# A DMA that adds, seven state buffers and a moved softplus in a one-core Mamba layer with experts

## The chip, the cores and the metric

The kernel runs on one core of a Trainium2 chip, as one launch. The metric is the device time in microseconds (us) from its start to its end. The engines of a core work side by side and meet only at semaphores: TensorE (PE in the profile, PEld for its weight loads), VectorE (DVE), ScalarE (ACT), GpSimd (POOL) and SyncE (SP), which here only issues loads. Sixteen DMA engines move the data.

## What is computed

A layer on x of 8 x 256 tokens with 1024 features. First an adapted projection (`cond`), then a selective state-space block with its scan over the tokens, then a second adapted projection folded into a layer of 8 low-rank experts of which each token uses 2. The scan is the part that matters here:

```
u, gate = split(cond(x) @ W_in.T)                    # 2048 channels each
u = silu(conv4(u) + conv_b)
dt, Bm, Cm = rmsnorm of the parts of u @ Wx.T        # 64, 16, 16
delta = softplus(dt @ Wdt.T + dt_bias)
state = exp(delta * A) * state + (delta * u) * Bm    # per token; 16 states per channel
y = sum over the 16 states of (state * Cm) + u * D
x = x + (y * silu(gate)) @ W_out.T
x = x + ffn(cond2(x))                                # top 2 of 8 experts of rank 64
```

All of it is float32. A matmul of 128 x 128 weights by 256 tokens stands in the trace as two rows.

## The kernel before

**Chunks.** Channels are taken 128 at a time and batch rows one at a time: 8 rows x 16 channel groups = 128 chunks, numbered `i`, with batch row `b = i // 16` and group `c = i % 16`. The 16 states of a chunk are taken in four quarters `q` of 4 states, each a tile of 128 partitions x 1024 (4 states x 256 tokens). A quarter has the number `n = 4 i + q`.

**One quarter.** GpSimd multiplies `delta * u` (`w_sb`, made once a chunk by `weight`) by the broadcast rows of B into a plane of the ring `st` (`dbu`, L1544). ScalarE writes `exp(delta * A)` into one of two PSUM tiles `scan0`, `scan1` (`decay`, L1146 and L1149). VectorE scans along the tokens in place (`scan`, L1317) and multiplies the result by the rows of C (`mul`).

**Adding the four products.** The product of q = 0 goes to its plane in `st`. That of q = 1 stays in PSUM (L1327), and `add_first` on VectorE adds the plane of q = 0 to it and writes the plane of q = 1 (L1334). The products of q = 2 and 3 go to their planes (L1329); GpSimd adds plane 1 into 2 and 2 into 3 (`add`, L1552), folds four states to two (`fold`, L1558), and TensorE sums the last two through the identity into PSUM (`sum_states`, L666). VectorE then makes `y` (`y_sum`, `y_gate`).

**The ring.** `st` has `ST_RING = 6` planes, taken round. A `dbu` may start when the plane it overwrites is free: for q = 2 that is `mul_done` of the chunk before, for q = 1 `id_mm`, TensorE's sum of two chunks earlier.

**Softplus.** `dt_proj` on TensorE leaves two channel groups (128 x 512) in a PSUM bank. ScalarE writes relu of it to `delta` and abs to `tmp` (`dt_evac`, L1032, L1033), which frees the bank, then exp and ln on `tmp` (`softplus`, L1039, L1041). GpSimd adds `tmp` to `delta` (`delta_add`, L1562). There are 64 of these, eight to a batch row.

**The other work of a chunk's turn (slot).** TensorE has in each slot a `late` job (mostly a 1024 x 256 piece of the output projection, 32 rows of the trace), a `small` and a `half` job, the sum of the chunk before, the `u` projection 20 chunks ahead and the gate projection of the next chunk (16 rows each). Each job uses one PSUM bank and waits until the job before in that bank is emptied. VectorE also does the three taps of the convolution (`conv_tap`, L1298) and adds results of the late and half jobs. Weight tiles of 512 KB go by SP into the ring `wt` of 6.

**What sets the order.** Each engine runs its own list, written out by hand in the loop over `i`; nothing is reordered. The order on VectorE in chunk `i` is: scan 0, late result, scan 1, the other results, product 0, product 1, `add_first`, scan 2, taps, scan 3, product 2, product 3, y of chunk `i - 1`. On GpSimd: `delta_add` if there is one, `weight(i + 1)`, `dbu` 0 to 2 of `i + 1`, add 2, add 3, fold of `i`, `dbu` 3 of `i + 1`.

## Time and profile before

| | us |
|---|---|
| median of 3 runs | 2437.41 (2436.84 to 2438.94) |
| time of the profiled execution | 2438.53 |
| span of its trace | 2436.6 |
| busy: PE, DVE, POOL, ACT | 2248.4, 2228.7, 2117.4, 1614.4 |
| prologue, up to the first scan | 119.7 |
| the 128 chunks | 2255.6 |
| tail, from the end of the last scan on | 61.3 |

Shares of the whole span mix a prologue with stages whose limits differ, so the table says only which engines come into question. What bounds a stretch is read from the stretch: the busy time of each engine in it, and whether an engine starts each instruction as the one before ends. Times of instructions are "start, duration"; two neighbours overlap by some 0.08 us, so the cost of one is taken from start to start.

### The profile page before, as it was taken

What the parts mean: (1) busy time and instruction counts of PE and PEld (TensorE: products, weight loads), DVE (VectorE), ACT (ScalarE), POOL (GpSimd) and SP (SyncE); (2) the same over time, 40 slices, a digit from 0 to 9 for tenths busy, and PEclk for the clock granted to TensorE, in tenths of its full rate; (3) what the DMA queues carried; (4) which work ended last, traced back from release to release, by engine and by line L of the source; (5) the groups of instructions that cost most, each with busy time, mean ns of one, the idle gap of its engine ahead of it and who ended that gap; (6) DMA issues with size and microseconds to landing.
All of it is one profiled execution on the core that took longest, in us unless ns stands there. A gap on an engine that the chain in (4) does not pass through costs nothing.

```text
span 2436.6 us, 30543 instructions
## 1 busy us (share of the span) xinstructions
PE 2248.4 (92%) x10140; PEld 1898.7 (78%) x10140; DVE 2228.7 (91%) x2104; ACT 1614.4 (66%) x3763; POOL 2117.4 (87%) x1090
## 2 busy tenths in 40 slices
PE   8999999999999999999999999999989887788879
PEld 7777878888788877888778877888768765666767
DVE  1389999999999999999999999999999999998892
ACT  1367667866677667776677667776677666765550
POOL 0189889999899999999899999999899989999870
PEclk9999999999999999999999999999989987998989
DMA  7454444433455344534454334644345332532342
GB/s 228 143 200 111 136 138 171 154 131 130 140 190 159 122 156 164 168 126 152 140 182 163 117 127 150 207 136 149 116 161 162 133 98 72 185 125 88 113 140 96
DMA packets 133178, 352.15 MB, mean 145 GB/s; under 512 B 38733, under 2 KB 43341, under 8 KB 131549
## 3 DMA queue, kind: packets, MB, share of 16 engines
q1 hardware_dynamic: 110254, 298.28, 37.1%
q10 hardware_dynamic: 22768, 51.93, 6.4%
q8 instruction: 81, 1.33, 0.2%
q14 instruction: 75, 0.61, 0.1%
HBM read 339.14 MB, written 11.02 MB: 144 GB/s over the span
## 4 chain that ended last, share of the span: by engine, by line
PE 32%; DVE 27%; POOL 19%; issue 12%; ACT 10%; ACTq 0%; DMA 0%; DVEq 0%; SPq 0%; POOLq 0%
DVE scan L1317 14%; POOL st L1544 10%; PE ubank L649 5%; POOL st L1552 5%; PE ubank L622 5%; PE late L703 5%; DVE st L1329 4%; DVE ubank L1298 3%; ACT scan L1149 3%; DVE scan L1327 3%; ACT L1238 3%; PE scan L622 2%; PE gbank L601 2%; ACT L1153 2%; POOL st L1558 1%
## 5 line engine op out<-in xcount | busy, mean ns | idle before, releaser
L1544 POOL TENSOR_TENSOR st<-w_sb,bc 128x1024 f32<-128x1024 f32 x512 | 1199.0, 2357 | 113.7 <-PE gbank L666 100.8
L1317 DVE TENSOR_TENSOR_SCAN scan<-scan,st 128x1024 f32<-128x1024 f32 x512 | 1167.5, 2288 | 35.6 <-POOL st L1544 23.5
L1149 ACT ACTIVATE scan<-delta,A_sb 128x255 f32<-128x255 f32 x2048 | 846.0, 459 | 0.1
L1552 POOL TENSOR_TENSOR st<-st 128x1024 f32<-128x1024 f32 x255 | 601.0, 2357 | 24.5 <-DVE st L1329 14.5
L649 PE MATMUL ubank<-h,wt 128*128 128x256 f32 x2048 | 473.4, 385 | 24.4 <-ACT qg L1238 24.1
L622 PE MATMUL ubank<-h,wt 128*128 128x256 f32 x1712 | 420.1, 402 | 77.3 <-ACT qg L1238 69.8
L649 PEld LDWEIGHTS ubank<-h,wt 128*128 128x128 f32 x2048 | 395.1, 193 | 84.0 <-ACT qg L1238 28.2
L622 PEld LDWEIGHTS ubank<-h,wt 128*128 128x128 f32 x1712 | 338.3, 201 | 153.7 <-ACT qg L1238 104.5
L1329 DVE TENSOR_TENSOR st<-scan,bc 128x1024 f32<-128x1024 f32 x384 | 453.7, 1207 | 0.0
L703 PE MATMUL late<-yg,wt 128*128 128x256 f32 x1792 | 407.3, 387 | 24.5 <-DVE x L1354 21.9
L703 PEld LDWEIGHTS late<-yg,wt 128*128 128x128 f32 x1792 | 347.4, 194 | 76.7 <-DVE x L1354 24.8
L1146 ACT ACTIVATE scan<-iota 128x4 f32<-128x4 f32 x512 | 86.8, 170 | 479.6 <-DVE st L1329 444.1
L1238 ACT ACT_TABLE_LOAD x128 | 164.2, 1283 | 172.7 <-DVE ubank L1298 167.6
L1562 POOL TENSOR_TENSOR delta<-delta,tmp 128x512 f32<-128x512 f32 x64 | 81.4, 1272 | 113.2 <-ACT tmp L1041 113.2
L1558 POOL TENSOR_TENSOR st<-st 128x512 f32<-128x512 f32 x127 | 161.4, 1271 | 10.0
L1153 ACT ACT_TABLE_LOAD x129 | 165.5, 1283 | 2.3
L666 PE MATMUL gbank<-st,ident 128*128 128x256 f32 x508 | 137.2, 393 | 30.4 <-POOL st L1558 12.6
L1298 DVE SCALAR_TENSOR_TENSOR ubank<-up,cw,ubank 128x256 f32<-128x256 f32 x321 | 154.6, 482 | 10.2 <-DVE wf L1419 1.5
L1334 DVE TENSOR_TENSOR st<-scan,st 128x1024 f32<-128x1024 f32 x128 | 156.6, 1223 | 4.1
L1327 DVE TENSOR_TENSOR scan<-scan,bc 128x1024 f32<-128x1024 f32 x128 | 156.2, 1220 | 0.0
L666 PEld LDWEIGHTS gbank<-st,ident 128*128 128x128 f32 x508 | 95.9, 194 | 52.2 <-issue 23.7
L601 PE MATMUL gbank<-xb,wt 128*128 128x256 f32 x512 | 121.3, 392 | 0.0
(221 smaller groups left out, 2332.1 us busy)
## 6 DMA issues: line engine op xcount, KB each, us to landing
wt<-in_W_in SPq DMA_DIRECT2D x256, 512.0 KB, 3.7
wt<-in_W_out SPq DMA_DIRECT2D x132, 512.0 KB, 3.7
wt<-in_cond_W SPq DMA_DIRECT2D x64, 512.0 KB, 3.6
bc<-bc_rows ACTq DMA_DIRECT2D x64, 512.0 KB, 6.6
wt<-G_tiles SPq DMA_DIRECT2D x32, 512.0 KB, 4.3
wt<-in_ffn_B SPq DMA_DIRECT2D x20, 512.0 KB, 3.7
xb<-in_x SPq DMA_DIRECT2D x8, 1024.0 KB, 6.1
x<-in_x ACTq DMA_DIRECT2D x28, 256.0 KB, 3.7
```

The lines of the kernel that those rows point to most:

```text
L622: last = mm(o[:, 0:T], wt[:, n % W_RING, k, :], h0[:, b % 3, k, :], start=(k == 0), stop=(k == KH - 1))
L649: last = mm(ubank[:, T:2 * T], wt[:, n % W_RING, k, :], h0[:, b % 3, k, :], start=(k == 0), stop=(k == KH - 1))
L666: last = mm(gbank[:, 0:T], ident[:, :], st[:, n % ST_RING, k, :], start=(k == 0), stop=(k == 1))
L703: last = mm(o, wt[:, n % W_RING, k, :], yg[:, (NC * f + h * KH + k) % Y_RING, :], start=(h == 0 and k == 0), stop=(h == 1 and k == KH - 1))
L1149: last = fn(t[:, k, 1:T], delta[:, c, 1:T], ACT.Exp, scale=A_sb[:, col:col + 1])
L1238: fn(qg[:, i % 2, :], ubank[:, T:2 * T], ACT.Silu).then_inc(q_done, 1)
L1298: v_.scalar_tensor_tensor(cv_home(v), up[:, e, k:k + T], cw[:, c, k:k + 1], cv_home(v), ALU.mult, ALU.add).then_inc(conv_step, 1)
L1317: v_.tensor_tensor_scan(Tps[q % 2][:, :], Tps[q % 2][:, :], x_, 0.0, ALU.mult, ALU.add).then_inc(scan_done, 1)
L1327: v_.tensor_tensor(Tps[1][:, :], Tps[1][:, :], cq, ALU.mult).then_inc(prod_done, 1)
L1329: v_.tensor_tensor(plane(n), Tps[q % 2][:, :], cq, ALU.mult).then_inc(mul_done, 1)
L1544: tt(st[:, n % ST_RING, :, :], w_sb[:, i % 2:i % 2 + 1, :].to_broadcast([P, NQ, T]), bc[:, 0, q * NQ:(q + 1) * NQ, :], ALU.mult).then_inc( ...
L1552: tt(st[:, n % ST_RING, :, :], st[:, n % ST_RING, :, :], st[:, (n - 1) % ST_RING, :, :], ALU.add).then_inc(add_done, 1)
```

## The change

Six things are changed together.

1. `add_first` is gone. Product 1 is written to its plane like the others (L1344 of the changed kernel), and GpSimd issues one DMA (`add_dma`, L1566) that adds plane 0 into plane 1 in SBUF. It waits for product 1. The add of q = 2 waits for that DMA (`acc_st[0]`).
2. The ring `st` has 7 planes. `dbu` 2 now waits for `id_mm`, `dbu` 3 for the DMA of the chunk before, and `dbu` 1 for nothing.
3. Softplus: ScalarE writes abs to `delta`, then exp and ln in place; VectorE finishes it with one instruction, max(x, 0) + `delta`, that reads the PSUM bank (`delta_sum`). The relu, `tmp` and GpSimd's `delta_add` are gone. The bank is freed only behind `delta_sum`.
4. On VectorE products 0 and 1 each stand behind their own scan; `delta_sum` stands behind scan 1. y stays last.
5. To make room: `sel` is gone, `weights_b` picks a column of the identity and makes each expert's 64 rows by a matmul of its own (two for one), and `wT` is a part of `la`, with a wait at `wT` and at the adapter for its other user.
6. Weight tiles of two `cond` jobs a batch row come as two half tiles.

```
-ST_RING = 6
+ST_RING = 7
...
             def weights_b(m, o):
-                return mm(o, sel[:, m * P:(m + 1) * P], wT[:, :], start=True, stop=True)
+                for e in range(2):
+                    pick = ident[0:E, 2 * m + e:2 * m + e + 1].to_broadcast([E, ER])
+                    last = mm(o[e * ER:(e + 1) * ER, :], pick, wT[:, :], start=True, stop=True)
+                return last
...
             def adapter(job):
                 act.wait_ge(*made(job))
+                if job[1] >= 4:
+                    act.wait_ge(*made(("wb", job[1] - 4, 1)))
...
-            def dt_evac(job):
...
-                fn(delta[:, 2 * j:2 * j + 2, :].rearrange("p c t -> p (c t)"), o, ACT.Relu)
-                fn(tmp[:, j % 2, :, :].rearrange("p c t -> p (c t)"), o, ACT.Abs).then_inc(ev_inc(job), 1)
...
+                flat = delta[:, 2 * j:2 * j + 2, :].rearrange("p c t -> p (c t)")
+                act.wait_ge(*made(("dt", b, j)))
+                fn(flat, home(("dt", b, j))[:, :], ACT.Abs).then_inc(sp_step, 1)
+                act.wait_ge(sp_step, 3 * n + 1)
                 fn(flat, flat, ACT.Exp, scale=-1.0).then_inc(sp_step, 1)
...
+            def delta_sum(b, j):
...
+                dve.wait_ge(sp_step, 3 * n + 3)
+                v_.scalar_tensor_tensor(d, home(job)[:, :], 0.0, d, ALU.max, ALU.add).then_inc(delta_done, 1)
+                dve.wait_ge(delta_done, n + 1)
+                dve.sem_inc(ev_inc(job), 1)
...
-            def add_first(i):
-                dve.wait_ge(prod_done, i + 1)
-                dve.wait_ge(mul_done, 4 * i + 1)
-                v_.tensor_tensor(plane(4 * i + 1), Tps[1][:, :], plane(4 * i), ALU.add).then_inc(mul_done, 1)
...
-                if q == 2 and i:
-                    pool.wait_ge(mul_done, 4 * i - 2)
-                if q == 1 and i >= 2:
+                if q == 2 and i >= 2:
                     pool.wait_ge(id_mm, i - 1)
+                if q == 3 and i:
+                    pool.wait_ge(acc_st[0], 16 * i)
...
+            def add_dma(i, k):
+                n = 4 * i + k
+                pool.wait_ge(mul_done, n + 1)
...
+                pool.dma_start(st[:, n % ST_RING, :, :], st[:, (n - 1) % ST_RING, :, :], accum_op=ALU.add
+                               ).then_inc(acc_st[k - 1], 16)
...
             def add(i, k):
                 n = 4 * i + k
-                if k == 3:
+                if k == 2:
+                    pool.wait_ge(acc_st[0], 16 * (i + 1))
+                else:
                     pool.wait_ge(add_done, 3 * i + 1)
```

On VectorE, one chunk in the middle of the program. `scan` is the pair of PSUM tiles, `x` the residual, `up` the input of the taps. Before:

```order
L1317 SCALAR_TENSOR_TENSOR scan<-scan,st 128x1024 [waits dbu_done,dA_done]
L1354 TENSOR_TENSOR x<-x,late 128x256 [waits late_mm]
L1317 SCALAR_TENSOR_TENSOR scan<-scan,st 128x1024 [waits dbu_done,dA_done]
L1329 TENSOR_TENSOR st<-scan,bc 128x1024 [waits scan_done]
L1327 TENSOR_TENSOR scan<-scan,bc 128x1024 [waits scan_done]
L1334 TENSOR_TENSOR st<-scan,st 128x1024 [waits mul_done,prod_done]
L1317 SCALAR_TENSOR_TENSOR scan<-scan,st 128x1024 [waits dbu_done,dA_done]
```

The same stretch of VectorE's list in the changed kernel:

```order
L1335 SCALAR_TENSOR_TENSOR scan<-scan,st 128x1024 [waits dbu_done,dA_done]
L1364 TENSOR_TENSOR x<-x,late 128x256 [waits x2_ld2,late_mm]
L1344 TENSOR_TENSOR st<-scan,bc 128x1024 [waits scan_done]
L1335 SCALAR_TENSOR_TENSOR scan<-scan,st 128x1024 [waits dbu_done,dA_done]
L1344 TENSOR_TENSOR st<-scan,bc 128x1024 [waits scan_done]
L1335 SCALAR_TENSOR_TENSOR scan<-scan,st 128x1024 [waits dbu_done,dA_done]
```

Product 0 moved ahead of the second scan, product 1 writes a plane of `st`, and the third instruction of 128 x 1024 is gone. In the chunks that finish a softplus, `delta_sum` stands between the second scan and its product.

On GpSimd, one turn of its loop in the middle of the program, with a softplus in it. Before:

```order
L1562 TENSOR_TENSOR delta<-delta,tmp 128x512 [waits sp_step]
L1531 TENSOR_TENSOR w_sb<-delta,u_sb 128x256 [waits u_done,dadd_done]
L1544 TENSOR_TENSOR st<-w_sb,bc 128x1024 [waits w_done]
L1544 TENSOR_TENSOR st<-w_sb,bc 128x1024 [waits id_mm]
L1544 TENSOR_TENSOR st<-w_sb,bc 128x1024 [waits mul_done]
L1552 TENSOR_TENSOR st<-st 128x1024 [waits mul_done]
L1552 TENSOR_TENSOR st<-st 128x1024 [waits mul_done,add_done]
L1558 TENSOR_TENSOR st<-st 128x512 [waits add_done]
L1544 TENSOR_TENSOR st<-w_sb,bc 128x1024
```

The same turn in the changed kernel:

```order
L1544 TENSOR_TENSOR w_sb<-delta,u_sb 128x256 [waits u_done,delta_done]
L1558 TENSOR_TENSOR st<-w_sb,bc 128x1024 [waits w_done]
L1566 DMA st<-st 128x1024 [waits mul_done]
L1558 TENSOR_TENSOR st<-w_sb,bc 128x1024
L1558 TENSOR_TENSOR st<-w_sb,bc 128x1024 [waits id_mm]
L1576 TENSOR_TENSOR st<-st 128x1024 [waits mul_done,acc_st0]
L1576 TENSOR_TENSOR st<-st 128x1024 [waits mul_done,add_done]
L1582 TENSOR_TENSOR st<-st 128x512 [waits add_done]
L1558 TENSOR_TENSOR st<-w_sb,bc 128x1024 [waits acc_st0]
```

The addition to `delta` left the list, a DMA entered it, two `dbu` ahead of the add that waits for it, and the waits for planes moved by one quarter.

## Rows read from the trace of the kernel before

**Rows 1.** Windows: length, busy (instructions) by engine, clock, DMA; batch rows 0, 1, 3, 6, 7

```profile
core 0: us, PE busy (x) PEld busy (x) DVE busy (x) ACT busy (x) POOL busy (x), PEclk, DMA share, GB/s
...
119.70:414.60 294.90, 277.06 (x1275) 236.20 (x1274) 272.26 (x233) 208.63 (x499) 262.67 (x135) 0.98 0.47 151
414.60:694.60 280.00, 271.43 (x1264) 231.18 (x1263) 274.47 (x256) 202.17 (x476) 266.39 (x138) 0.99 0.45 148
...
973.70:1253.70 280.00, 267.74 (x1227) 227.22 (x1226) 276.70 (x262) 200.12 (x469) 266.14 (x138) 0.98 0.46 151
...
1812.90:2089.30 276.40, 238.01 (x1020) 197.35 (x1020) 273.35 (x252) 193.56 (x449) 260.99 (x135) 0.91 0.39 128
2089.30:2375.30 286.00, 235.73 (x993) 195.60 (x991) 258.62 (x225) 171.90 (x392) 259.37 (x133) 0.92 0.37 123
```

**Rows 2.** Timeline of DVE in chunk 61: start, duration, what, idle before it

```profile
1205.54 1.21 DVE L1329 TENSOR_TENSOR st<-scan,bc 128x1024 f32<-128x1024 f32 x1
1206.66 1.22 DVE L1327 TENSOR_TENSOR scan<-scan,bc 128x1024 f32<-128x1024 f32 x1
1207.91 1.23 DVE L1334 TENSOR_TENSOR st<-scan,st 128x1024 f32<-128x1024 f32 x1
1209.05 2.29 DVE L1317 TENSOR_TENSOR_SCAN scan<-scan,st 128x1024 f32<-128x1024 f32 x1
...
1212.67 0.48 DVE L1304 SCALAR_TENSOR_TENSOR xs<-xs,lnw,small 97x256 f32<-97x256 f32 x1
1213.36 2.30 DVE L1317 TENSOR_TENSOR_SCAN scan<-scan,st 128x1024 f32<-128x1024 f32 x1 [0.21 <-DVE xs L1304]
```

**Rows 3.** Timeline of POOL in batch row 7, chunks 118 and 119

```profile
2189.52 0.73 POOL L1531 TENSOR_TENSOR w_sb<-delta,u_sb 128x256 f32<-128x256 f32 x1
...
2206.88 0.73 POOL L1531 TENSOR_TENSOR w_sb<-delta,u_sb 128x256 f32<-128x256 f32 x1
2207.68 6.98 POOL L1544 TENSOR_TENSOR st<-w_sb,bc 128x1024 f32<-128x1024 f32 x3
2214.61 4.80 POOL L1552 TENSOR_TENSOR st<-st 128x1024 f32<-128x1024 f32 x2
...
2223.00 0.73 POOL L1531 TENSOR_TENSOR w_sb<-delta,u_sb 128x256 f32<-128x256 f32 x1
```

**Rows 4.** Windows: the first eight chunks of batch row 7

```profile
2089.30:2228.50 139.20, 112.38 (x461) 93.09 (x459) 128.12 (x102) 93.01 (x210) 137.32 (x73) 0.92 0.40 128
```

**Rows 5.** Waits in those eight chunks: us, times, longest

```profile
DVE scan L1317 <- POOL st L1544: 10.5, 8, 1.5
```

**Rows 6.** Timeline of PE: sixteen rows and what follows them

```profile
1201.77 3.62 PE L649 MATMUL ubank<-h,wt 128*128 128x256 f32 x16
1205.22 0.60 PE L684 MATMUL small<-sq,mean_w 97*97 97x256 f32 x2
```

**Rows 7.** Groups by line: count, busy, mean ns, idle before

```profile
L1562 POOL TENSOR_TENSOR delta<-delta,tmp 128x512 f32<-128x512 f32 x64 | 81.4, 1272 | 113.2 <-ACT tmp L1041 113.2
L1358 DVE TENSOR_TENSOR hw<-hw,late 128x512 f32<-128x512 f32 x14 | 9.4, 673 | 0.0
L1340 DVE SCALAR_TENSOR_TENSOR gbank<-u_sb,D_sb,gbank 128x256 f32<-128x256 f32 x128 | 61.3, 479 | 12.8 <-PE gbank L605 10.6 <-PE gbank L931 2.0
L1354 DVE TENSOR_TENSOR x<-x,late 128x256 f32<-128x256 f32 x56 | 22.7, 405 | 0.0
```

**Rows 8.** DMA issues: count, KB each, median us from issue to landing

```profile
wt<-in_W_in SPq DMA_DIRECT2D x256, 512.0 KB, 3.7
bc<-bc_rows ACTq DMA_DIRECT2D x64, 512.0 KB, 6.6
...
xb<-in_x SPq DMA_DIRECT2D x8, 1024.0 KB, 6.1
```

**Rows 9.** Timeline of SP: one issue, its duration second

```profile
1220.00 0.33 SPq L493 DMA_DIRECT2D wt<-in_cond_W  x1
```

**Rows 10.** Waits of POOL over the whole span: us, times, longest

```profile
POOL st L1544 <- PE gbank L666: 100.8, 56, 10.3
```

## What I expect, and why

> **What bounds the kernel now.** I read the busy table first: TensorE, VectorE and GpSimd are all near 90% of the span, so it decides nothing. Then I cut the span at the first scan of each batch row and read the busy times by window. In row 3, which stands for rows 2 to 5 (279.1 to 280.0 us each), VectorE is busy 276.7 of 280.0 us, TensorE 267.7, GpSimd 266.1 [rows 1]. In VectorE's timeline each instruction starts as the last one ends [rows 2], so these rows are VectorE's: 280.0 / 16 = 17.50 us a chunk. Row 0 is different: it has more matmul rows, 1275 in 294.9 us, most of them in its first eleven chunks, and neither VectorE (272.3) nor GpSimd (262.7) fills it [rows 1]. Row 7 is different again: in its first eight chunks GpSimd is busy 137.3 of 139.2 us, VectorE 128.1 [rows 4], and VectorE waits for GpSimd once in each of them, 10.5 us in all [rows 5]. There the chunk takes what GpSimd's list takes, 17.36 us with a `delta_add` (from 2189.52 to 2206.88) and 16.12 without (2206.88 to 2223.00) [rows 3]. That is the useful finding: GpSimd's own work is 16.12 us a chunk, plus 1.24 for each `delta_add`, and when it is the slowest nothing else is added.
>
> TensorE's work: 16 rows take 3.45 us from start to start, 0.216 each [rows 6]; row 3 has 1227 [rows 1], so 264.6 us or 16.5 a chunk. All three engines are within 6% of each other. A change that relieves one is worth at most the distance to the next.
>
> **VectorE.** Product 1 and `add_first` take 2.39 us (1206.66 to 1209.05) and a lone product 1.12 (1205.54 to 1206.66) [rows 2]: 1.27 us a chunk go. A product right behind its own scan has to wait for it: a dependent instruction starts 0.03 us after the end of the one before (L1334), an independent one 0.08 to 0.09 before it [rows 2], so 0.12 for each of the two where nothing stands between; late results and `delta_sum` stand between in most chunks, and I take 0.1 a chunk. `delta_sum` is 128 x 512 with a PSUM input: 0.67 us for two inputs, and the three-operand form of 128 x 256 takes 0.48 where the two-operand one takes 0.41 [rows 7], so about 0.75. Behind it stands a wait for itself and an increment, as behind the norm, where the next scan starts 0.21 us after the end [rows 2]: 0.96 in all, eight times a batch row, 0.48 a chunk. Sum: 17.50 - 1.27 + 0.1 + 0.48 = **16.8 us a chunk**.
>
> **GpSimd.** `delta_add` goes: 64 of 1.27 us [rows 7]. The issue of the DMA comes in, and no row shows GpSimd issuing one. Below, 0.33 us, which an issue costs SP [rows 9]; a gain is excluded, since an instruction is added. Above, 1.27 us, its pass over 128 x 512 [rows 7]. GpSimd builds the 128 rows' descriptors itself, so I stay near its own small instructions, between its 0.73 for 128 x 256 [rows 3] and that 1.27, and take 1.0. Sum: 16.12 + 1.0 = **17.1 us a chunk**, if the DMA has landed in time.
>
> The Trainium skill (DMA: Bandwidth & Descriptors, Specifications) gives a first-byte latency of about 1 us for a DMA issued from GpSimd; no run here shows it yet. By that figure as the issue cost, an estimate, the sum is the same.
>
> **The DMA.** It waits for product 1, which VectorE now finishes about halfway through the chunk (two scans and two products, 2 x 2.2 + 2 x 1.12 and a late result [rows 2]). GpSimd comes to it one `dbu` after `weight(i + 1)`, and if GpSimd is the slowest it comes late to everything: this wait should be empty. What is queued behind it are two `dbu`, 6.93 x 2/3 = 4.62 us [rows 3], and then the add that needs the result. So what shows is the landing time, counted from the end of the issue, beyond 4.62 us. A load of the same 512 KB lands 3.7 us after its issue begins; one of 1024 KB takes 6.1, and the slowest 512 KB, the broadcast of B and C, 6.6 [rows 8]. With the issue of 0.33 [rows 9] taken off these are 3.4, 5.8 and 6.3, so the visible wait is between 0 and 1.7 us. I take 0, because the load of the same size is nearest, and keep the upper end.
>
> **The seventh plane** moves the wait for TensorE's sum from `dbu` 1 to `dbu` 2, 2.3 us later. GpSimd waited 100.8 us there [rows 10], but in rows where VectorE set the pace, so this is slack that will be eaten by the new issue rather than a gain. It also is what puts two `dbu` and not one ahead of the add. The new wait of `dbu` 3 for the last DMA is behind an add that already waited for it: nothing.
>
> **TensorE and ScalarE.** `weights_b` doubles its matmuls: 8 more rows a batch row, 8 x 0.216 = 1.7 us, which makes 16.6 us a chunk. The bank of `dt` is freed by VectorE behind scan 1, some 7 us into the chunk, and no longer by ScalarE near its start; behind it waits the next `small` job, and behind that TensorE's whole list. In a slot with a late job of 32 rows (32 x 0.216 = 6.9 us) TensorE comes there later than that. Slots 0 to 5 of row 0 and slot 14 have no such job, and 1 to 2 us may show in each, in slots with few rows. The adapter's new wait comes behind the longest slot (13). I count 1 us a batch row for these. ScalarE loses a relu, 64 times; it has 80 us of idle time per batch row [rows 1], so nothing. Half tiles: nothing, loads run five tiles ahead.
>
> **The sum,** with 17.12 us a chunk, GpSimd's: rows 2 to 5 from 279.6 to 273.9 + 1, 4.7 each, 19 together; row 1 from 280.0 to 275, 5; row 6 from 276.4 to 274.5, 2; row 7, first eight chunks from 139.2 to 137.0, 2, the next one back 1, and the rest, where TensorE's slots hold up to 92 rows (19.8 us) with the last row's output projection, unchanged; row 0, whose 1275 rows alone are 275 us and bunched, 0 to 1, with the start (VectorE's 0.75 in place of GpSimd's 1.27 ahead of the first scan). Together 27 to 28. The profiled execution's 2438.5 becomes 2411; the median of the runs is 1 us below that execution, which is nothing here. **Predicted: 2411 us**, its own range 2395 to 2430.
>
> **Rivals.** (a) *Cheap issue.* If the issue costs 0.33 us and the DMA lands in time, GpSimd needs 16.5 and VectorE's 16.8 is the bound, with TensorE at 16.6 beside it. Rows 1 to 5 save 10 us each, row 6 6, the first half of row 7 8, row 0 3: 67 us, **2371**. For it speaks only SP's issue [rows 9].
>
> (b) *The landing shows,* the slower side. It decides at GpSimd's add of q = 2. One microsecond more a chunk costs some 115 us, because about 115 chunks then go at GpSimd's pace (not the TensorE-bound ones of rows 0 and 7). Against a gain of 27 us the point is 27 / 115 = 0.23 us: if issue and visible wait together pass **1.24 us**, the kernel is slower. With a landing as of 1024 KB and an issue of 1.0, the wait is 5.8 - 4.62 = 1.2 us and the time 2411 + 138 = **2549**; halfway, 0.6 us, it is 2480. For it: the DMA engines are 45% busy in these rows [rows 1], and an add has to read both planes. Against it: source and target are both in SBUF, and the 3.7 us are for a read from memory under the same load.
>
> The Trainium skill (Collectives: The Full Stack, The bandwidth ceiling) has the rule that speaks against this change: an add done by a DMA reads two sources and so moves its bytes at about half the rate of a copy. No row here shows an adding DMA; by that rule the price is that of the 1024 KB row, and the time that of (b).
>
> (c) *No net change.* The VectorE time is freed as said, and GpSimd's issue takes it: an issue of 1.15 to 1.3 us with no wait gives 2430 to 2443.
>
> (d) *The three lists jam.* With all three within 3% of each other, TensorE's long slots no longer hide under VectorE's longer chunks. By its jobs slot 9 has 16 + 36 + 4 + 32 = 88 rows and slot 13 has 2 + 36 + 4 + 16 + 4 + 32 = 94, 19.0 and 20.3 us. How much lag the banks allow no row shows. Priced above at 1 us; at 3 us a batch row it would be 16 us, 2427. I count it within the forecast's range.
>
> **How the numbers follow.** Forecast 0.42; (a) 0.15; (c) 0.10, nearly all of it within the bound; (b) 0.33, of which 0.2 below 2500. A measurement of this kernel can tell about 0.2%, 5 us, from no change. Faster is forecast and (a): 0.57. Same 0.09. Slower 0.34. The range 2368 to 2500 leaves out the far part of (b), some 0.13, and a little below. As both signs hold much of the chance, the forecast's own 2395 to 2430 stands beside it.
>
> **What would show it.** Right: in row 3 GpSimd is the one busy without gaps, at 17.1 us from `weight` to `weight`; VectorE waits for L1558 once a chunk; the add of q = 2 starts without a wait on the DMA; VectorE's busy time in row 3 falls to about 266 us; a DMA issue on GpSimd near 1.0 us. Wrong by (b): idle time ahead of L1576 ended by the DMA, landings above 5.6 us from the start of the issue. Wrong by (a): chunks at 16.8 and no wait of VectorE on GpSimd. Wrong in a way I have not priced: GpSimd's other instructions or the weight loads get longer while the new DMA runs, or TensorE waits in slots 0 to 5 for `small`.

## The result: 0.2% slower, and where the chunk's time is now

The changed kernel takes **2444.13 us** in the median of 19 runs (2438.47 to 2449.45; one disturbed run, 2479.9, is left out of these limits and of the ratio), the kernel before 2438.66 (19 runs, 2436.84 to 2442.09): a ratio of 1.0021, 95% interval 1.0015 to 1.0028. Forecast were 2411 us and faster. The time is inside the wide range of 2368 to 2500, outside the forecast's own of 2395 to 2430, and the direction is wrong.

The profile of the changed kernel: what answers [rows 7], [rows 8] and the busy table (in the groups: busy us, mean ns of one, idle time just before and what ended it).

```profile
PE 2253.2 (92%) x10204; PEld 1899.9 (78%) x10204; DVE 2138.3 (87%) x2040; ACT 1593.1 (65%) x3699; POOL 2149.7 (88%) x1154
POOL 70%; PE 12%; issue 9%; DVE 6%; ACT 2%; DMA 0%; POOLq 0%; ACTq 0%; SPq 0%; DVEq 0%
L1576 POOL TENSOR_TENSOR st<-st 128x1024 f32<-128x1024 f32 x255 | 616.0, 2416 | 75.7 <-DMA st<-st 60.1
L1566 POOL DMA_DIRECT2D st<-st x128 | 112.2, 876 | 0.0
wt<-in_W_in SPq DMA_DIRECT2D x256, 512.0 KB, 4.2
st<-st POOLq DMA_DIRECT2D x128, 512.0 KB, 5.3
```

The second line is the chain that ended last, by engine: 70% of it is GpSimd. The adding DMA lands 5.3 us after its issue begins, and the add that needs it (L1576) has 75.7 us of idle time before it, of which 60.1 are ended by that DMA. Most other loads land a little later than they did, W_in after 4.2 us where it was 3.7.

Batch rows 0, 1, 3, 6 and 7 in windows, as in [rows 1]:

```profile
core 0: us, PE busy (x) PEld busy (x) DVE busy (x) ACT busy (x) POOL busy (x), PEclk, DMA share, GB/s
120.20:417.20 297.00, 279.38 (x1285) 237.88 (x1284) 261.00 (x225) 205.64 (x491) 265.96 (x143) 0.98 0.62 176
417.20:699.00 281.80, 270.07 (x1272) 230.01 (x1271) 263.50 (x248) 199.70 (x467) 269.83 (x145) 0.99 0.61 178
...
979.90:1262.60 282.70, 270.25 (x1235) 229.46 (x1234) 265.54 (x254) 197.84 (x460) 268.40 (x145) 0.97 0.61 179
...
1827.00:2104.60 277.60, 238.85 (x1028) 197.24 (x1028) 261.93 (x244) 191.08 (x442) 268.73 (x145) 0.92 0.54 157
2104.60:2386.90 282.30, 234.73 (x1002) 193.78 (x1000) 244.04 (x215) 169.44 (x386) 264.44 (x142) 0.93 0.55 154
```

In row 3 VectorE is busy 265.5 us where it was 276.7, as forecast (266). Yet the row takes 282.7 us and not 275, and no engine fills it: GpSimd is busy 268.4 of it, TensorE 270.3. 14 us of GpSimd's time are gaps. The DMA engines are busy 61% of it, from 46%.

GpSimd in two stretches: undisturbed, late in row 6, and in chunk 12 of row 7.

```profile
2031.05 0.72 POOL L1544 TENSOR_TENSOR w_sb<-delta,u_sb 128x256 f32<-128x256 f32 x1
2031.85 2.34 POOL L1558 TENSOR_TENSOR st<-w_sb,bc 128x1024 f32<-128x1024 f32 x1
2034.13 0.87 POOL L1566 DMA_DIRECT2D st<-st  x1
2034.74 4.96 POOL L1558 TENSOR_TENSOR st<-w_sb,bc 128x1024 f32<-128x1024 f32 x2
2039.37 5.05 POOL L1576 TENSOR_TENSOR st<-st 128x1024 f32<-128x1024 f32 x2
...
2048.04 0.72 POOL L1544 TENSOR_TENSOR w_sb<-delta,u_sb 128x256 f32<-128x256 f32 x1
...
2315.92 0.87 POOL L1566 DMA_DIRECT2D st<-st  x1
2316.52 4.97 POOL L1558 TENSOR_TENSOR st<-w_sb,bc 128x1024 f32<-128x1024 f32 x2
2325.03 4.78 POOL L1576 TENSOR_TENSOR st<-st 128x1024 f32<-128x1024 f32 x2 [3.54 <-DMA st<-st]
```

The first stretch is the forecast come true: 16.99 us from `weight` to `weight` (2031.05 to 2048.04; forecast 17.1), where [rows 3] had 16.12. The issue's row is 0.87 us long, but the next `dbu` starts 0.61 us after it; the rest comes later, since the two adds take 5.05 us where they take 4.78 behind a wait. Together 0.9 us for an issue. Counted from the start of the issue, the add comes after 2039.37 - 2034.13 = 5.24 us. That is the whole cover, the time in which the transfer can land unseen, and the median landing is 5.3 us. The second stretch shows what follows when it is later: the two `dbu` are done and GpSimd stands for 3.54 us.

The waits, over the whole span (us, times, longest):

```profile
DVE scan L1335 <- POOL st L1558: 91.5, 73, 3.9
PE gbank L679 <- POOL st L1582: 60.9, 28, 5.3
POOL st L1576 <- DMA st<-st: 60.1, 44, 4.8
POOL st L1558 <- PE gbank L679: 30.0, 12, 9.3
PE small L689 <- DMA wt<-in_Wx: 10.9, 4, 3.4
```

VectorE waits for GpSimd 73 times and not once in each of the 128 chunks. The last row is a wait that the kernel before has nowhere. The wait for TensorE's sum, 100.8 us in [rows 10], is down to 30.0.

### The profile page after: what moved, and what is told of

Same layout as the page of the kernel before. It is cut to its first block, busy times and chain, and to the rows that moved or that the text cites. A ratio compares the mean times of both kernels' runs of the same rounds, so it can differ in the third digit from the quotient of the medians.

```text
span 2444.8 us, 30623 instructions
## 1 busy us (share of the span) xinstructions
PE 2253.2 (92%) x10204; PEld 1899.9 (78%) x10204; DVE 2138.3 (87%) x2040; ACT 1593.1 (65%) x3699; POOL 2149.7 (88%) x1154
## 4 chain that ended last, share of the span: by engine, by line
POOL 70%; PE 12%; issue 9%; DVE 6%; ACT 2%; DMA 0%; POOLq 0%; ACTq 0%; SPq 0%; DVEq 0%
POOL st L1558 38%; POOL st L1576 22%; POOL st L1582 5%; DVE scan L1335 4%; POOL w_sb L1544 3%; POOL st L1566 2%; PE scan L635 2%; PE gbank L614 1%; PE scan L614 1%; PE ubank L662 1%; PE ubank L635 1%; DVE st L1344 1%; PE small L763 1%; PE late L764 1%; ACT scan L1160 1%
## 5 line engine op out<-in xcount | busy, mean ns | idle before, releaser
L1558 POOL TENSOR_TENSOR st<-w_sb,bc 128x1024 f32<-128x1024 f32 x512 | 1238.2, 2494 | 42.5 <-PE gbank L679 30.0
L1576 POOL TENSOR_TENSOR st<-st 128x1024 f32<-128x1024 f32 x255 | 616.0, 2416 | 75.7 <-DMA st<-st 60.1
L1344 DVE TENSOR_TENSOR st<-scan,bc 128x1024 f32<-128x1024 f32 x512 | 611.3, 1214 | 11.0 <-DVE delta L1323 2.4
L662 PE MATMUL ubank<-h,wt 128*128 128x256 f32 x2048 | 469.5, 383 | 5.1 <-ACT qg L1247 5.1
L635 PE MATMUL ubank<-h,wt 128*128 128x256 f32 x1712 | 410.0, 395 | 39.4 <-ACT qg L1247 34.4
L679 PE MATMUL gbank<-st,ident 128*128 128x256 f32 x508 | 146.8, 415 | 66.9 <-POOL st L1582 60.9
L1544 POOL TENSOR_TENSOR w_sb<-delta,u_sb 128x256 f32<-128x256 f32 x128 | 93.0, 727 | 114.4 <-DVE delta L1323 114.4
L614 PEld LDWEIGHTS gbank<-xb,wt 128*128 128x128 f32 x512 | 101.6, 199 | 15.2
L1566 POOL DMA_DIRECT2D st<-st x128 | 112.2, 876 | 0.0
```

What stands on the lines that cost most here:

```text
L614: mm(o, wt[:, n % W_RING, k - first, :], xb[:, k, :], start=(k == 0), stop=False)
L635: last = mm(o[:, 0:T], wt[:, n % W_RING, k, :], h0[:, b % 3, k, :], start=(k == 0), stop=(k == KH - 1))
L662: last = mm(ubank[:, T:2 * T], wt[:, n % W_RING, k, :], h0[:, b % 3, k, :], start=(k == 0), stop=(k == KH - 1))
L679: last = mm(gbank[:, 0:T], ident[:, :], st[:, n % ST_RING, k, :], start=(k == 0), stop=(k == 1))
L1344: v_.tensor_tensor(plane(n), Tps[q % 2][:, :], cq, ALU.mult).then_inc(mul_done, 1)
L1544: tt(w_sb[:, i % 2, :], delta[:, c, :], u_sb[:, i % U_RING, :], ALU.mult).then_inc(w_done, 1)
```

## Experiments

Three theories stood at the start. A: the changed kernel loses its gain to the late landing of the adding DMA and what TensorE loses behind it. B: the landing costs nothing, the issue is the whole price. C: the gain is lost to the other edits (order on VectorE, bank of `dt`, `weights_b`). The kernel before ran beside each set, at medians of 2437.25 us (e1 to e4), 2437.86 (e5 to e8), 2438.59 (e9 to e11) and 2439.87 (e12).

**e1, no addition.** The DMA and its waits go, and product 0 is left out of the sum.

```
-                    pool.wait_ge(acc_st[0], 16 * i)
+                    pool.wait_ge(mul_done, 4 * i - 3)
...
-                if k == 2:
-                    pool.wait_ge(acc_st[0], 16 * (i + 1))
-                else:
+                if k == 3:
...
-                add_dma(i, 1)
```

> The changed kernel without its adding DMA and the waits for it; product 0 is therefore left out of the sum over the states. Three theories. A, the landing: GpSimd keeps a steady 17.02 us a chunk with the DMA, and the gain over 17.50 is lost where the DMA lands late (54.6 us of waits in 44 chunks) and in what TensorE loses behind those stalls. B, the issue: 0.9 us of GpSimd's list a chunk is the whole cost, landing hardly matters. C, the other edits (softplus on VectorE, order of products, two matmuls for one in weights_b, half tiles) cost the gain. A and B both expect GpSimd at 16.1 us a chunk, VectorE (16.6 busy) the bound, 2375 to 2400 us. C expects this kernel to stay above 2415.

Measured: 2356.65 us (2352.2 to 2361.64), ratio 0.9675 (0.9656 to 0.9695). The DMA costs 87 us in all, more than A or B expected. C falls as the whole cause: without the DMA the other edits leave a kernel far below the one before. Its batch rows 2 to 5 take 268.7 to 269.7 us, 16.8 a chunk.

**e2, a quarter of the bytes.** The issue stays; the DMA adds one of four states (128 KB).

```
-                pool.dma_start(st[:, n % ST_RING, :, :], st[:, (n - 1) % ST_RING, :, :], accum_op=ALU.add
+                pool.dma_start(st[:, n % ST_RING, 0:1, :], st[:, (n - 1) % ST_RING, 0:1, :], accum_op=ALU.add
```

> The changed kernel with a DMA that adds only the first of the four states of the plane, 128 KB for 512 KB (three quarters of product 0 are left out of the sum). Issue on GpSimd stays near 0.9 us, landing falls from 5.3 to about 3 us, well inside the 5.2 us from the issue's start to the add. A expects the waits on the DMA to vanish and 2385 to 2405 us. B expects no more than 10 us off 2444. C expects above 2425.

Measured: 2394.08 us (2389.62 to 2396.11), ratio 0.9821 (0.9805 to 0.9838). Its landing and the wait for it:

```profile
st<-st POOLq DMA_DIRECT2D x128, 128.0 KB, 3.3
```

```profile
POOL st L1576 <- DMA st<-st: 4.6, 7, 1.3
```

So the 87 us split: 37 for the issue with a short transfer (e1 to e2) and 50 for what the full transfer adds (e2 to the changed kernel). The time is where A had it, and B falls.

**e3, the addition back on VectorE,** everything else as changed.

```
+                if q == 1:
+                    v_.tensor_tensor(Tps[1][:, :], Tps[1][:, :], cq, ALU.mult).then_inc(prod_done, 1)
...
+            def add_first(i):
+                dve.wait_ge(prod_done, i + 1)
+                dve.wait_ge(mul_done, 4 * i + 1)
+                v_.tensor_tensor(plane(4 * i + 1), Tps[1][:, :], plane(4 * i), ALU.add).then_inc(mul_done, 1)
...
                 mul(i, 1)
+                add_first(i)
...
-                add_dma(i, 1)
```

> The changed kernel with the addition back on VectorE, product 1 in PSUM and add_first right behind it, everything else of the change kept. All theories: VectorE is the bound, busy 16.6 + 1.27 = 17.9 us a chunk against 17.3 before, so about 2438 + 115 x 0.45 = 2490 us. C expects over 2505, since its losses come on top.

Measured: 2480.72 us (2479.67 to 2482.24), ratio 1.0177 (1.016 to 1.0194). It is below what was expected, and C's 2505 is not reached. Beside e1 this gives the books of the change: the other edits, with VectorE still the bound, cost 43 us, which no run splits further (the prediction had counted 0.58 us a chunk for them on VectorE); taking the addition from VectorE gives 124 back; the DMA takes 87. The net is 7 us slower (beside its own runs of the kernel before it is 5).

**e4, the last pair first.** GpSimd adds plane 2 to 3 first and plane 1, the DMA's, second, so that an add more covers the landing: 7.9 us from the start of the issue in place of 5.2, in the median of its trace. The work is the same and so is the result.

```
-                n = 4 * i + k
-                if k == 2:
+                swapped = i + 1 < CHUNKS
+                n = 4 * i + (3 if swapped else k)
+                src = 4 * i + ((2 if k == 2 else 1) if swapped else k - 1)
+                if k == (3 if swapped else 2):
                     pool.wait_ge(acc_st[0], 16 * (i + 1))
-                else:
+                if k == 3:
                     pool.wait_ge(add_done, 3 * i + 1)
...
-                tt(st[:, n % ST_RING, :, :], st[:, n % ST_RING, :, :], st[:, (n - 1) % ST_RING, :, :], ALU.add
+                tt(st[:, n % ST_RING, :, :], st[:, n % ST_RING, :, :], st[:, src % ST_RING, :, :], ALU.add
```

> The changed kernel with GpSimd's two adds of a chunk exchanged: first plane 2 into plane 3, then plane 1, which the DMA made, into plane 3. Same instructions and same bytes, but the DMA now has two dbu and one add, 7.0 us, ahead of its reader instead of 4.6. A expects nearly all waits on the DMA gone (only landings over 7.6 us from the issue remain, under a tenth of them) and 2390 to 2410 us. B expects 2440 to 2445. C expects above 2425.

Measured: **2406.07 us** (2403.1 to 2409.34), ratio 0.9868 (0.9852 to 0.9884). The wait on the transfer, which itself lands no earlier (5.4 us):

```profile
POOL st L1578 <- DMA st<-st: 13.6, 9, 5.9
```

46 us of waiting less, 38 us of time less, within A's range. A is shown for these 38 us: same bytes, same issue, and only the order of the two adds and with it the place of the wait differs.

**e5, the softmax order.** In batch row 3, chunks 11 and 12, which carry part of the softmax, take 38.34 us together where they took 36.11 before. This run and the next ask why; theory D is that the moved softmax steps do it.

```
+                if weigh:
+                    soft_max_step(b - 1, 4)
                 scan(i, 2)
                 if weigh:
-                    soft_max_step(b - 1, 4)
+                    soft_max_step(b - 1, 5)
...
-                if weigh:
-                    soft_max_step(b - 1, 5)
```

> The changed kernel, with VectorE's softmax steps 4 and 5 back in the place that they have in the kernel before (step 4 ahead of the third scan, step 5 right behind it and ahead of the taps). In the changed kernel the three softmax chunks c10 to c12 of a batch row take 56.7 us where they took 53.4 before. Theory A (landing of the adding DMA; the softmax chunks are slow from TensorE, whose fold wait and Wx tiles come late): nothing changes, 2441 to 2446 us. Rival D (the weights wf come late by the moved step 5, and everything from the gate weights on shifts): 3 us a batch row in six rows come back, 2424 to 2432 us.

Measured: 2442.14 us (2439.78 to 2449.84), ratio 1.0023 (1.0014 to 1.0033). Nothing changes; D falls.

**e6, the Wx tiles first.**

```
+                tiles = slot_tiles(i)
+                if tiles[0][0] == "wx":
+                    load_tile(tiles[0])
+                    load_tile(tiles[1])
+                    tiles = tiles[2:]
                 if c == (13 if b == 0 else 12) and b + 3 < B:
...
-                for t in slot_tiles(i):
+                for t in tiles:
```

> The changed kernel, with SyncE issuing chunk c12's two Wx tiles ahead of its wait for the last half of the conditioning (made cond 7) and the loads behind that wait; nothing else moves. The trace shows TensorE waiting for Wx four times, 10.9 us in all, once in each of b1 to b4, with nothing of the kind before. Theory E (these waits are on the path: the products for dt and B/C come late, VectorE and GpSimd wait 3.4 and 3.1 us behind them): 2.5 to 3 us for each of four rows, 2432 to 2436 us. Rival (GpSimd is behind by its own late transfer at that place, so a tile in time only moves the wait): 2441 to 2445 us.

Measured: 2443.14 us (2431.27 to 2450.89, 10 runs), ratio 1.0016 (0.9999 to 1.0034). The profiled execution, 2434.5, is among the fastest of them. In it the waits for Wx are gone, yet the median has moved by less than these runs can tell. By the median the rival would hold, but the ten runs spread over both expectations. On this kernel the test is inconclusive; e11 repeats it where fewer late transfers scatter the time. What the wait is, is seen in TensorE's timeline of the changed kernel, row 3, chunks 11 and 12, and in SyncE's:

```profile
1181.90 2.08 PE L679 MATMUL gbank<-st,ident 128*128 128x256 f32 x4 [2.90 <-POOL st L1582]
1183.77 5.67 PE L614 MATMUL gbank<-xb,wt 128*128 128x256 f32 x16
1189.28 0.59 PE L618 MATMUL gbank<-la,cB 128*128 128x256 f32 x2
...
1201.24 8.37 PE L689 MATMUL small<-u_sb,wt 128*97 128x256 f32 x30 [2.72 <-DMA wt<-in_Wx]
```

```profile
1195.17 0.89 SPq L499 DMA_DIRECT2D wt<-in_Wx  x2
```

TensorE waits 2.90 us for GpSimd's sum, then the sixteen rows of the last half of the conditioning take 5.67 us where sixteen rows take 3.62 elsewhere ([rows 6]), and with the two rows behind them end at 1189.9. SyncE waits for just these rows before it loads the next conditioning, and the two Wx tiles are queued behind that. So here a late sum turns into a late load, and the load into a wait of its own one chunk on. In the kernel before, the Wx tiles were issued 3.1 us ahead of the start of chunk 12 (1183.73); here 3.1 us behind it (1192.04). Row 3 is the worst of the four: in rows 1, 2 and 4 the first of the two tiles is issued between 0.2 us ahead of that start and 1.4 us behind it.

The landing of the adding DMA is not what this hangs on. The same wait in e4, where few landings are late, and in e1, without the DMA and with no wait of TensorE for the sum in these chunks:

```profile
PE small L689 <- DMA wt<-in_Wx: 14.0, 4, 4.1
```

```profile
PE small L689 <- DMA wt<-in_Wx: 5.3, 4, 1.8
```

Of the runs with the changed kernel's load order only e3, in which VectorE still sets the pace, has no wait for Wx. So half of the 10.9 us is there without any DMA, and a late sum can only add to it. That the shorter chunks make the tiles late is the likely reason for that half; no run isolates it.

**e8, less beside the DMA.** Left out are the broadcast rows of B and C of batch rows 1 to 7.

```
+                w = QT if b == 0 else 4
+                act.dma_start(bc[:, which, q * NQ:(q + 1) * NQ, :].rearrange("p n t -> p (n t)")[:, 0:w],
+                              src[:, 0:w].to_broadcast([P, w])).then_inc((B_ld, C_ld)[which][q], 16)
```

> Left out: the rows of B and C broadcast for batch rows 1 to 7 (each of these 56 loads of 512 KB brings four elements a partition in place of 1024, so that row 0's values are used on); everything that waits for them still does. Theory A (the adding DMA is late where other loads run beside it): the 12 late waits of GpSimd in c15 and c0 of the rows, 19.8 us together, go, and the time is 2420 to 2428 us. Rival (the adding DMA's landing is its own, 5.3 us whatever runs beside it; the waits are there for a different reason): they stay, 2440 to 2445 us.

Measured: 2433.93 us (2426.3 to 2440.41), ratio 0.9981 (0.997 to 0.9993). This is between the two expectations. The late waits fall from 60.1 to 37.8 us; in the trace, those in chunk 15 and the chunk 0 behind it from 19.8 to 5.8 us (9 of 12 left, shorter), and those in the other chunks from 35.5 to 25.2. The rest, 4.8 and 6.8 us, is the very last chunk, in which no `dbu` covers the transfer. So the broadcast loads do make the DMA late, and the time falls by 10 us where 16 to 24 were expected. What makes it late in the other chunks is not shown; other loads are the likely cause.

**e11, swapped pairs and Wx first; e7, these and the softmax order.** Their edits are those of e4, e6 and e5.

> The swapped pairs of e4 (2406.1 us there), the softmax order of e5 and the Wx order of e6 together. If the costs are separate they add up: 2406 less 10 for Wx (four waits of 14.0 us in e4) less nothing for the softmax order, 2393 to 2399 us. If GpSimd's steady 17.1 us a chunk is the floor in the softmax chunks too, 2402 to 2407 us.

> e7 without the softmax order: the swapped pairs (2406.1 us by themselves) and the Wx tiles ahead of the wait for the conditioning. If the 8 us from e4 to e7 are the Wx order's alone, 2395 to 2401 us; if they are the softmax order's, 2403 to 2408 us.

Measured: e7 2397.76 us (2395.47 to 2404.16), ratio 0.9843 (0.9827 to 0.986); e11 **2398.15 us** (2396.57 to 2399.7), ratio 0.9833 (0.9817 to 0.9849). The softmax order is nothing again. Against e4 the Wx order brings 8 us; the intervals of the two ratios are 0.0003 apart, and the times of their runs do not overlap. In the traces batch rows 1 to 4, the four with the wait for Wx, are 3.2, 1.2, 4.0 and 3.5 us shorter than in e4, and row 5 is not. Of e11, the same stretch of TensorE:

```profile
1164.87 1.13 PE L684 MATMUL gbank<-st,ident 128*128 128x256 f32 x4 [2.37 <-POOL st L1589]
1165.84 3.62 PE L619 MATMUL gbank<-xb,wt 128*128 128x256 f32 x16
...
1179.34 6.72 PE L694 MATMUL small<-u_sb,wt 128*97 128x256 f32 x30
```

and its batch rows 0, 1, 3, 6 and 7:

```profile
119.80:417.90 298.10, 280.87 (x1285) 239.30 (x1284) 261.00 (x224) 205.57 (x490) 266.59 (x143) 0.97 0.60 175
417.90:692.00 274.10, 267.66 (x1272) 228.64 (x1271) 263.04 (x248) 199.68 (x468) 268.37 (x145) 1.00 0.61 182
966.80:1241.40 274.60, 263.69 (x1235) 223.93 (x1234) 265.21 (x253) 197.52 (x459) 268.48 (x145) 1.00 0.63 186
1790.20:2063.30 273.10, 233.96 (x1025) 194.65 (x1025) 261.16 (x244) 190.95 (x441) 268.12 (x145) 0.93 0.55 160
2063.30:2337.00 273.70, 232.59 (x1000) 193.73 (x999) 243.73 (x214) 169.07 (x386) 264.20 (x142) 0.93 0.53 157
```

Rows 1, 3 and 6 were forecast at 275, 274.9 and 274.5 us.

**e10, the DMA one `dbu` later.** On the changed kernel: the cover is 2.3 us shorter.

```
                     dbu(i + 1, 0)
+                if not last:
+                    dbu(i + 1, 1)
                 add_dma(i, 1)
                 if not last:
-                    dbu(i + 1, 1)
                     dbu(i + 1, 2)
```

> The changed kernel with the adding DMA issued behind the dB*u of the second quarter in place of ahead of it, so that 2.3 us less of GpSimd's work covers its landing (2.9 us from the start of the issue in place of 5.2). Theory A (the landing, 5.3 us in the median from the start of the issue, is waited for wherever the cover ends): GpSimd waits 2.3 to 2.5 us in nearly every chunk where it waited 0.5 us in the mean, 1.9 us by some 120 chunks, 2640 to 2700 us. Theory B (issue is the whole cost): 2440 to 2450 us.

Measured: 2708.58 us (2699.2 to 2714.67), ratio 1.1095 (1.107 to 1.112).

```profile
POOL st L1576 <- DMA st<-st: 329.4, 121, 7.6
```

2.7 us in each of 121 chunks, a little above the 2.3 to 2.5 expected, and the time 9 us above its range. Against the changed kernel it is 264 us of time for 269 us of waiting. With e4 and the changed kernel this makes three points for one transfer of 5.3 to 5.5 us: a cover of 7.9 us leaves 13.6 us of waiting, 5.2 leaves 60.1, 2.9 leaves 329.4.

**e9, two half transfers; e12, the same with more scratch space.** Both on e7.

```
-                pool.dma_start(st[:, n % ST_RING, :, :], st[:, (n - 1) % ST_RING, :, :], accum_op=ALU.add
-                               ).then_inc(acc_st[k - 1], 16)
+                for h in (0, 2):
+                    pool.dma_start(st[:, n % ST_RING, h:h + 2, :], st[:, (n - 1) % ST_RING, h:h + 2, :], accum_op=ALU.add
+                                   ).then_inc(acc_st[k - 1], 16)
```

> e7 (2397.8 us: swapped pairs, softmax order, Wx order), with GpSimd's addition of the first two products issued as two transfers of 256 KB in place of one of 512 KB; the same bytes, and a cover of 7 us in which e7's late waits are 12.6 us in all. It prices an issue by itself. Theory F (an issue costs GpSimd what the rows of the changed kernel give, 0.61 us from its start to the next start and 0.28 us that its queue catches up with behind, once for the pair): 0.61 to 0.88 us in each of some 120 chunks in which GpSimd sets the pace, 2470 to 2505 us. Rival (a second issue hides in GpSimd's queue): below 2415 us.

Measured: 2674.86 us (2661.9 to 2678.49), ratio 1.0954 (1.092 to 1.0987), far outside either expectation. GpSimd in two chunks of it:

```profile
914.84 0.88 POOL L1572 DMA_DIRECT2D st<-st  x1
918.58 0.85 POOL L1572 DMA_DIRECT2D st<-st  x1 [2.86 <-issue]
919.14 4.99 POOL L1563 TENSOR_TENSOR st<-w_sb,bc 128x1024 f32<-128x1024 f32 x2
...
950.51 0.73 POOL L1549 TENSOR_TENSOR w_sb<-delta,u_sb 128x256 f32<-128x256 f32 x1
...
953.60 1.76 POOL L1572 DMA_DIRECT2D st<-st  x2
...
968.49 0.73 POOL L1549 TENSOR_TENSOR w_sb<-delta,u_sb 128x256 f32<-128x256 f32 x1
```

In the later chunk the pair goes through: 17.98 us from `weight` to `weight` (950.51 to 968.49), 0.9 above e7's pace, theory F's size. In the earlier one the second issue starts 2.86 us after the end of the first, and the profile names nothing that it waited for. In the waits:

```profile
POOL st L1572 <- issue: 186.2, 55, 7.0
```

e12 changes one number, `dynamic_dma_scratch_size=1024` to 4096.

> e9 (two adding transfers of 256 KB in a row, 2674.9 us), with the scratch space for GpSimd's own transfers at 4096 bytes a partition in place of 1024 (dynamic_dma_scratch_size); nothing else differs. In e9 the second issue begins 3 to 4.5 us late in 55 chunks, 186 us in all, with nothing that the profile shows to wait for; in the other chunks the pair costs GpSimd 0.85 us more than one transfer. Theory G (the second issue waits for room in that space, which the first transfer gives back as it lands): the 186 us go, and 0.85 us by 128 chunks above e7's 2397.8 stay, 2490 to 2515 us. Rival (GpSimd issues no second transfer while the first is under way in these chunks, whatever the space): 2660 to 2690 us.

Measured: 2528.32 us (2524.24 to 2530.43), ratio 1.0354 (1.0336 to 1.0373), and

```profile
POOL st L1572 <- issue: 23.5, 8, 3.6
```

G is right in the main: with four times the space 163 of the 186 us are gone, so the space for GpSimd's own transfers was full. The time is 13 us above its range; 8 such waits are left, with 21.8 us on the landing of the second half (12.6 in e7), and what the 8 wait for stays open. The second issue then costs (2528 - 2398) / 128 = 1.0 us a chunk with these waits in it, and some 0.8 without them, as an estimate.

## Why the prediction was wrong

**The step that failed** is the one on the landing. It put the wait of GpSimd's add for the adding DMA between 0 and 1.7 us a chunk and took 0, because the load of the same size (3.7 us) was nearest. The chip gives 5.3 us from the start of the issue, between that row and the 1024 KB row (6.1), with a wait of 60.1 / 128 = 0.47 us a chunk in the mean. The prediction had the rule to price it: 115 us for each microsecond, 54 us here, where e4 gives 38 and e2 50. It had the break-even too, 1.24 us for issue and visible wait together; they came to 0.9 + 0.47 = 1.37, by that rule 15 us slower than before, and it is 5. So rival (b) is what happened, near its lower end. A second fault is in the reasoning: it compared median landings with the cover, as if a transfer whose median lies inside it cost nothing. In the trace a quarter of the 128 landings are above 6.0 us, one in ten above 7.1, and most of each late one is paid, since GpSimd has little slack to give back (38 us of time for 46 of waiting in e4, 264 for 269 in e10). A third is in the bounds: they took SP's 0.33 us off the landings for the issue, where the sum itself had 1.0 for it and the trace gives 0.61 until the next `dbu` starts.

By DMA queue, the changed kernel's trace shows packets, MB and their share of the 16 engines' time, for SyncE's loads and for the adding DMA:

```profile
q1 hardware_dynamic: 111678, 298.27, 37.4%
q0 software_dynamic: 18432, 67.12, 14.9%
```

For each MB the adding DMA holds the engines 1.8 times as long. A packet of 4 KB takes 328 ns of an engine in the median, one of the loads 159 ns. On the rule that an add in a reduction reads two sources and so runs at about half a copy's rate (the Trainium skill, Collectives: The Full Stack, The bandwidth ceiling, which has it for a collective): these rows agree, though the loads beside it come from memory and no run here copies within SBUF without adding. In landings, from 128 KB in 3.3 us to 512 KB in 5.3 us, 384 KB more take 2.0 us, 197 GB/s. The fit of the Trainium skill for a transfer issued from GpSimd (DMA: Bandwidth & Descriptors, Anatomy of one DMA) has a fixed 2.0 us and 436 GB/s; half that rate is 218. As an estimate it would have given 2.0 + 2.4 = 4.4 us for 512 KB in an empty machine, 0.9 below what the traces show beside other loads, and inside the cover of 5.2. So the halved rate alone would not have foretold the wait either; by this estimate, what was missing is the time that other loads add.

**Not in the forecast at all** was the wait for Wx in chunk 12 of rows 1 to 4: the tiles are issued behind a wait for rows of TensorE that now end late. It was held at "loads run five tiles ahead" and 1 us a batch row for TensorE. It is 10.9 us of waiting in the four rows, and e11 against e4 gives 8 us in time. It does not come from the landing: e4 has it in full, e1 half of it.

**What was right,** shown by e11, in which most of these two causes is taken away (13.1 us on the landing are left): rows 1 to 6 take 273.1 to 274.8 us, forecast 274.5 to 275. GpSimd's pace (17.0 for 17.1) and the issue (0.9 for 1.0) were right, as was VectorE's busy time in row 3 (265.5 for 266); and e1, with GpSimd relieved, runs at the 16.8 us a chunk that the sum had for VectorE. The first-byte figure of about 1 us for a transfer issued from GpSimd (the Trainium skill, DMA: Bandwidth & Descriptors, Specifications) stood beside the 1.0 as if it were the engine's cost; the traces give 0.9 for the engine and 3.3 us until even 128 KB have landed. No run here shows the first byte, so the likeness is no evidence.

**Two terms were off and cancelled in part.** Row 0 takes 297.0 us in the changed kernel and 298.1 in e11, forecast 294 to 295. Row 7 was forecast at 285, with its second half unchanged because TensorE's long slots set it; the changed kernel takes 282.3 and e11 273.7, and from chunk 8 on e11 takes 137.1 us where it was 146.8. So TensorE's rows did not bind there as the count of rows had it. In the changed kernel row 7's 3 us less and row 0's 2 to 3 us more than forecast cancel, which is luck. No run isolates row 7's part.

Rival (a) needed an issue of 0.33 us: wrong. Rival (c) names the time almost exactly, 2430 to 2443, but by another cause: it wanted an issue of 1.15 to 1.3 us and no wait. Rival (d), the three lists jamming, is close to what chunk 12 shows, through a load and not through the row counts of slots 9 and 13.

## What to carry to other kernels

When an engine hands an addition to a DMA, compare the landing's upper tail, not its median, with the work queued ahead of the instruction that needs it, and place that instruction last among those that can be swapped: here the same two adds in the other order are worth 38 us. When chunks get shorter or an engine falls behind, loads that a queue issues behind a wait for that engine come late too; keep tiles that are needed next ahead of such a wait (8 us here). Both together turn a change that loses 0.2% into one that gains 1.7% (e11, 2398.15 us, below both kernels).

## What the runs showed of the hardware

- An issue on GpSimd has a row of 0.88 us, and the next instruction starts after 0.61; the remaining 0.28 us show as longer rows until the next wait (adds of 2.65 us where 2.36 is usual). Taken together, 0.9 us.
- The space for GpSimd's own transfers can be full with one transfer of 256 KB under way: the second issue then stands 2.5 to 7.0 us, 2.9 in the median, 55 times and 186.2 us in all in e9, and the profile shows it as idle time with no releaser. With 4096 bytes in place of 1024 it is 23.5 us (e12).
- An adding DMA within SBUF takes 328 ns of a DMA engine for a packet of 4 KB in the median, a load on SyncE's queue 159 ns, in the same trace.
- TensorE's granted clock after an idle stretch, in the changed kernel:

```profile
1178.40:1181.90 3.50, 0.60 (x3) 0.19 (x1) 3.50 (x6) 1.03 (x4) 3.42 (x3) 0.89 0.00 0
1181.90:1184.00 2.10, 2.10 (x5) 1.74 (x6) 2.10 (x4) 1.56 (x4) 2.10 (x1) 0.50 0.00 0
1184.00:1187.00 3.00, 3.00 (x8) 2.38 (x8) 2.61 (x8) 0.78 (x1) 2.92 (x3) 0.50 0.00 0
1187.00:1189.00 2.00, 2.00 (x8) 1.69 (x8) 2.00 (x2) 1.97 (x4) 2.00 (x3) 0.77 0.24 47
1189.00:1192.00 3.00, 3.00 (x17) 2.18 (x16) 2.97 (x5) 2.24 (x7) 3.00 (x2) 1.00 0.76 149
```

TensorE had been idle since 1179.0. The clock fell to 0.50, the level of 1.2 GHz, at 1181.1, within this wait of 2.90 us, and came back at 1187.9, so that eight rows took 3 us. After the wait of 2.91 us at the same place in e6, and after the 2.37 in e11, it stayed at full speed (3.62 us for the sixteen rows). What tells these cases apart is open; a short wait can cost as much again in slow rows, and need not.
